# Cross-attention and a feed-forward block: query rows on other partitions, whole key tables from TensorE, the second mask half copied on the chip, one product per turn of maxima, and a new order

## The reference, cut to what matters

```python
x = x + xattn(layernorm(x), ctx, mask)     # x: (2, 1024, 256), ctx: (2, 77, 256), 16 heads of 16
x = x + ffn(layernorm(x))

def xattn(x, y, mask):
    q, k, v = x @ Wq + bq, y @ Wk + bk, y @ Wv + bv
    att = einsum('bthd,bThd->bhtT', q, k) / 4
    att = softmax(att * mask - 1e10 * (1 - mask))
    return einsum('bhtT,bThd->bthd', att, v) @ Wo + bo

def ffn(t):                                # only expert 0 has weight; F = 1024
    z = t + relu(t @ w1[0] + b1[0]) @ w2[0] + b2[0]
    return layernorm(z) * gamma + beta
```

## Time and profile before

| | |
|---|---|
| median of 3 runs | 226.63 us |
| the profiled execution | 226.6 us, of which span 224.8 us |
| PE busy | 198.1 us (88%), 1264 instructions |
| DVE, ACT, POOL busy | 148.7, 119.8, 80.8 us |
| DMA moved | 23.99 MB in 14267 packets |
| chain that ended last | PE 65%, DMA 18%, SyncE's queue 7% |

### The profile page before, as it was taken

The page is one execution under the profiler, slowest core; times in us unless marked ns, Lnnn a source line. Parts: engine busy times, 40 slices in busy tenths (PEclk is TensorE's granted clock), DMA queues, the critical chain, the costliest instruction groups (busy, mean ns, idle before and its releaser), DMA issues.

```text
span 224.8 us, 3534 instructions
## 1 busy us (share of the span) xinstructions
PE 198.1 (88%) x1264; PEld 153.4 (68%) x1264; DVE 148.7 (66%) x345; ACT 119.8 (53%) x216; POOL 80.8 (36%) x87
## 2 busy tenths in 40 slices
PE   0399979869968699798999999999999999999991
PEld 0376565437535557475879696667998899988990
DVE  0999999753936957454487219249664397895774
ACT  3298525826757085757725648986024960159200
POOL 4367952710000100598230104932245453371121
PEclk9999999967999999999999999999999999999999
DMA  6994498790999953995002230202000011010012
GB/s 216 382 358 141 152 242 187 140 260 0 208 211 230 211 130 73 156 175 110 5 1 74 71 70 4 73 0 96 0 0 3 0 48 47 3 47 0 3 70 70
DMA packets 14267, 23.99 MB, mean 107 GB/s; under 512 B 1716, under 2 KB 5300, under 8 KB 14250
## 3 DMA queue, kind: packets, MB, share of 16 engines
q1 hardware_dynamic: 13274, 22.71, 40.6%
q10 hardware_dynamic: 976, 1.06, 1.6%
HBM read 16.56 MB, written 6.55 MB: 103 GB/s over the span
## 4 chain that ended last, share of the span: by engine, by line
PE 65%; DMA 18%; SPq 7%; ACT 3%; issue 3%; DVE 2%; ACTq 0%; POOLq 0%; POOL 0%
DMA Sq<-nmx 7%; PE W L765 7%; PE W L768 6%; PE W L766 6%; PE acc L701 5%; PE W L751 5%; PE W L752 5%; PE W L753 5%; PE T L689 5%; DMA wk<-in_L_xattn_Wk_dram 3%; DMA wo<-in_L_xattn_Wo_dram 3%; DMA Sq<-qD 3%; PE M L668 2%; PE W L710 2%; DMA Mq<-qD 2%
## 5 line engine op out<-in xcount | busy, mean ns | idle before, releaser
L865 ACT ACTIVATE PT<-T 77x512 f32<-77x512 f32 x64 | 36.0, 591 | 21.8 <-PE T L689 20.2
L1005 DVE TENSOR_REDUCE mx<-M 128x6 f32<-128x462 f32 (+1 forms) x48 | 26.7, 579 | 19.9 <-PE M L668 19.7
L765 PE MATMUL W<-w2h,hh 128*128 128x256 f32 x128 | 36.6, 286 | 0.4 <-DVE aTl L1023 0.4
L768 PE MATMUL W<-w2h,hl 128*128 128x256 f32 x128 | 36.1, 282 | 0.0
L766 PE MATMUL W<-w2l,hh 128*128 128x256 f32 x128 | 36.1, 282 | 0.0
L689 PE MATMUL T<-Sq,KS 128*77 128x512 f32 x64 | 25.6, 431 | 7.7 <-DMA Sq<-nmx 5.5
L1180 POOL TENSOR_TENSOR hl<-hr,hh 128x512 fp32r<-128x512 f32 x12 | 16.1, 1338 | 43.6 <-ACT hh L911 43.6
L907 ACT ACTIVATE hr<-W,cst 128x512 f32<-128x512 f32 x32 | 22.0, 687 | 16.6 <-PE W L753 15.5
L751 PE MATMUL W<-x2h,w1h 128*128 128x512 f32 x64 | 25.8, 403 | 0.0
L765 PEld LDWEIGHTS W<-w2h,hh 128*128 128x128 f32 x128 | 24.1, 189 | 1.7 <-issue 1.5
L752 PE MATMUL W<-x2l,w1h 128*128 128x512 f32 x64 | 25.2, 394 | 0.0
(11 more groups left out here) (122 smaller groups left out, 407.9 us busy)
## 6 DMA issues: line engine op xcount, KB each, us to landing
Sq<-qD SPq DMA_DIRECT2D x16, 256.0 KB
xin<-in_x_dram SPq DMA_DIRECT2D x4, 512.0 KB, 7.5
qD<-qh SPq DMA_DIRECT2D x8, 256.0 KB, 3.7
qD<-ql SPq DMA_DIRECT2D x8, 256.0 KB, 3.6
Sq<-qD SPq DMA_DIRECT2D x16, 128.0 KB
out_dram<-xn SPq DMA_DIRECT2D x6, 256.0 KB, 2.0
Mq<-qD SPq DMA_DIRECT2D x6, 192.0 KB, 4.8
w1raw<-in_L_ffn_w_dram SPq DMA_DIRECT2D x2, 512.0 KB, 11.3
```

The source lines that it names most:

```text
L765: e.matmul(y, hh[:, f, q:q + 128], w2h[:, f * E:(f + 1) * E], start=(f == 0), stop=False)
L768: i = e.matmul(y, hl[:, f, q:q + 128], w2h[:, f * E:(f + 1) * E], start=False, stop=(f == 7))
L865: e.activation(PT[:, m % 6, :], T[m % 2][0:TK, :], ACT.Exp).then_inc(exped, 1)
L1005: e.tensor_reduce(heads, M[(nth[step] - 1) % 2][:, 0:w * KP].rearrange("p (g h t) -> p g h t", g=1 if s < 2 else 2, t=KP)[:, :, :, 0:TK], ...
```

## The change

- The query rows move from partitions 64 to 111 to partitions 32 to 79 (`Q0`, `Q1`).
- `qD` holds three rows a query element: high, low, high. The high rows are written twice by one DMA (512 KB in place of 256), and each quad is loaded by one `Sq<-qD` DMA of 48 partitions in place of two.
- The key tables are made whole by TensorE: a bfloat16 unit product (12 new matmuls of 468 or 312 columns) starts each group, and the selection products, now 128 partitions wide, add the keys. The unit copies of ScalarE and GpSimd are gone; the copies out of PSUM cover 128 partitions. A small unit tile `eyer` is made by GpSimd.
- `mD` and its nine DMAs are gone; GpSimd copies the second mask half from `mT1` into the slots (six copies "maskm", eight "masks"). Three of the six "mslot" copies go from VectorE to GpSimd.
- "mxt" is one matmul with a negated unit matrix in place of four transposes. `nmx` then has 32 partitions of 128 and its DMA moves 16 pieces of 512 B in place of 4 of 2 KB.
- The first 512 KB of x come in two halves, one on SyncE's queue and one on ScalarE's ahead of `cst`; `wo` and `b2` are loaded early.
- `TIMES` is new for every engine.

The diff, cut to its core (of `TIMES` two lines):

```diff
-Q0 = 64
-Q1 = 112
+Q0 = 32
+Q1 = 80
...
-        "mslot": "15.0 15.5 16.0",
-        "maskm": "49.7 56.0",
+        "maskm": "43.3 45.2 48.4 49.1 50.2 51.0",
...
-        qD = [dram(f"qD{c}", (H, D, 2, 512)) for c in range(NC)]
+        qD = [dram(f"qD{c}", (H, D, 3, 512)) for c in range(NC)]
...
-            e.dma_start(xin[:, 0:4, :], x_v[:, row0(0)]).then_inc(ld_x[0], 16)
+            e.dma_start(xin[:, 0:2, :], x_v[:, row0(0), 0:2]).then_inc(ld_x0[0], 16)
...
-                    for p, q in ((0, Q0), (Q1, MR)):
-                        e.dma_start(Mqf[p:q, first:first + n, :], mD[p:q, :].unsqueeze(1).to_broadcast([q - p, n, 512])
-                                    ).then_inc(ms_new[i], 16)
...
-                    e.dma_start(qD[c][8 * g:8 * g + 8, :, 0, :].rearrange("h d n -> (h d) n"),
-                                qh[:, 2 * (c % 2) + g, :].bitcast(F32)).then_inc(qh_out[2 * (c % 2) + g], 16)
+                    e.dma_start(qD[c][8 * g:8 * g + 8, :, 0:3:2, :].rearrange("h d r n -> (h d) r n"),
+                                qh[:, 2 * (c % 2) + g, :].bitcast(F32).unsqueeze(1).to_broadcast([P, 2, 512])
+                                ).then_inc(qh_out[2 * (c % 2) + g], 16)
...
-                    e.dma_start(Sqf[Q0:Q0 + 32, s:s + 4, :], heads.rearrange("h d r n -> (d r) h n")).then_inc(sq_ld[u % 2], 16)
-                    e.dma_start(Sqf[Q0 + 32:Q1, s:s + 4, :],
-                                heads[:, :, 0, :].rearrange("h d n -> d h n")).then_inc(sq_ld[u % 2], 16)
+                    e.dma_start(Sqf[Q0:Q1, s:s + 4, :], heads.rearrange("h d r n -> (d r) h n")).then_inc(sq_ld[u % 2], 16)
...
-                    e.dma_start(Sqf[MR:MR + 1, s:s + 4, :], source.bitcast(F32)).then_inc(sq_ld[u % 2], 16)
+                    e.dma_start(Sqf[MR:MR + 1, s:s + 4, :].rearrange("p h (n t) -> p (h n) t", n=4),
+                                nmx[4 * s:4 * s + 16, k // 2, :].bitcast(F32)).then_inc(sq_ld[u % 2], 16)
...
+                    e.matmul(t[:, 0:2 * KP * len(heads)], identb[:, :], eyer[:, 0:2 * len(heads), :],
+                             start=True, stop=False)
...
+                            made = e.matmul(o, sel_m[:, h, :], high, start=False, stop=last)
...
-                    for n in range(4):
-                        i = e.transpose(t[0:r, n * 128:(n + 1) * 128], mx[:, c % 2, n, r * g:r * g + r], ident)
-                    i.then_inc(mx_turned, 1)
+                    e.matmul(t[0:32, 0:P], mx[:, c % 2, 8 * g:8 * g + 8, :].rearrange("p h n -> p (h n)"), identn[:, :],
+                             start=True, stop=True).then_inc(mx_turned, 1)
...
+            e.dma_start(xin[:, 2:4, :], x_v[:, row0(0), 2:4]).then_inc(ld_x0[1], 16)
             e.dma_start(cst[:, :], const).then_inc(ld_c, 16)
...
+                elif kind == "maskm":
+                    i, = a
+                    fresh.wait_ge(mT_made, 2)
+                    fresh.wait_ge(scored, nth["smax", 1, 3, (0, 2, 1)[i // 2]])
+                    e.tensor_copy(Mq[:, FREED[i], :], mT1[:, :].bitcast(F32)).then_inc(ms_new, 1)
+                elif kind == "masks":
+                    s, = a
+                    fresh.wait_ge(mT_made, 2)
+                    fresh.wait_ge(st_made, nth["st", 1, 8 + s])
+                    e.tensor_copy(Sq[:, s, :], mT1[:, :].bitcast(F32)).then_inc(sq_new, 1)
```

More of the change, by code:

```diff
@@ L139, in members @@
 def members(kind):
-    if kind in ("consts", "eyem", "sel", "flags", "crow", "bqr", "bk4", "mask", "splitwo", "statics"):
+    if kind in ("consts", "eyer", "sel", "flags", "crow", "bqr", "bk4", "mask", "splitwo"):
         return [[(kind,)]]
@@ L146, in members @@
         return [[(kind, to, g, j) for to in ("KM", "KS") for g in range(2) for j in range(3)]]
-    if kind in ("late", "ksid", "mslot", "sslot", "maskm", "masks"):
-        return [[(kind, i) for i in range({"late": 2, "ksid": 4, "mslot": 6, "sslot": 8, "maskm": 2, "masks": 2}[kind])]]
+    if kind in ("late", "mslot", "sslot", "maskm", "masks"):
+        return [[(kind, i) for i in range({"late": 4, "mslot": 6, "sslot": 8, "maskm": 6, "masks": 8}[kind])]]
     if kind == "split":
@@ L153, in members @@
     if kind == "mxt":
-        return [[(kind, c, g) for g in range(turns(c))] for c in range(NC)]
+        return [[(kind, c, g) for g in range(2)] for c in range(NC)]
     if kind in ("qproj", "qlow", "qload", "attn"):
@@ L168, in members @@
     return [[(kind, c)] for c in range(NC)]
-def turns(c):
-    return 2
-def turned_by(c, k):
-    return sum(turns(i) for i in range(c)) + (k // 2 + 1 if turns(c) == 2 else 1)
 def pool_takes(step):
@@ L206, in has_part @@
     if step[0] == "mslot":
-        return (step[1] < 3) == (engine == "DVE")
+        return (step[1] < MSLOT_POOL) == (engine == "POOL")
     if step[0] == "low":
@@ L212, in has_part @@
     return True
-KINDS = ("consts", "eyem", "sel", "flags", "crow", "bqr", "bk4", "kproj", "mask", "mT", "values", "ksid", "mslot", "sslot",
-         "keys", "split", "splitwo", "statics", "late", "maskm", "masks", "norm", "scale", "turn", "xbias", "qproj", "qlow",
+KINDS = ("consts", "eyer", "sel", "flags", "crow", "bqr", "bk4", "kproj", "mask", "mT", "values", "mslot", "sslot",
+         "keys", "split", "splitwo", "late", "maskm", "masks", "norm", "scale", "turn", "xbias", "qproj", "qlow",
          "qload", "smax", "mxt", "quadq", "quadm", "st", "pv", "weigh", "attn", "proj", "scale2", "turn2", "bias2", "ffn1",
@@ L290, in build @@
         ql = sb("ql", [P, 2, 512], F32R)
-        mx = sb("mx", [P, 2, 4, H])
-        nmx = sb("nmx", [H, 2, 512], F32R)
-        PT = sb("PT", [TK, 6, 512])
+        mx = sb("mx", [P, 2, H, 4], F32R)
+        identn = sb("identn", [P, P], F32R)
+        mT1 = sb("mT1", [P, 512], F32R)
+        with ExitStack() as over:
+            sel_m, sel_h, sel_l = (over.enter_context(nc.sbuf_tensor(name, [P, 8, P], F32R))
+                                   for name in ("sel_m", "sel_h", "sel_l"))
+        PT = sb("PT", [P, 6, 512])
+        nmx = PT[96:P, 0, 0:256].bitcast(F32R).rearrange("p (g t) -> p g t", g=2)
         pvq = sb("pvq", [P, 2, 512])
@@ L346, in build @@
         K3 = [T[0], T[1], acc]
-        ld_x = [sem(f"ld_x{c}") for c in range(NC)]
+        mT = [mT0, mT1]
+        ld_x0, ld_x = [sem("ld_x0a"), sem("ld_x0b")], [None] + [sem(f"ld_x{c}") for c in range(1, NC)]
         ld_c, ld_ctx, ld_wk, ld_m = sem("ld_c"), sem("ld_ctx"), sem("ld_wk"), sem("ld_m")
@@ L563, in sync_program @@
                     u, s = quad(c, k), 4 * (k % 2)
-                    fresh.wait_ge(nmx_made, turned_by(c, k))
+                    fresh.wait_ge(nmx_made, nth["mxt", c, k // 2])
                     if u < 2:
@@ L607, in tensor_program @@
                     fresh.wait_ge(mT_made, half(c) + 1)
-                    e.matmul(t[:, :], bqr[:, g, :], mT[:, 512 * half(c):512 * half(c) + 512],
-                             start=False, stop=True).then_inc(q_made, 1)
+                    e.matmul(t[:, :], bqr[:, g, :], mT[half(c)][:, :], start=False, stop=True).then_inc(q_made, 1)
                 elif kind == "kproj":
@@ L781, in scalar_program @@
                 kind, a = step[0], step[1:]
-                if kind == "eyem":
-                    fresh.wait_ge(ld_c, 16)
-                    for k in range(2):
-                        i = e.copy(KM[:, 8 * k:8 * k + 8, :, :].rearrange("p h b t -> p (h b) t"),
-                                   eye.unsqueeze(1).to_broadcast([P, H, KP]))
-                    i.then_inc(km_ident, 1)
-                elif kind == "sel":
+                if kind == "sel":
                     fresh.wait_ge(ld_c, 16)
```

168 lines of the change are left out of this document (76 added, 92 removed), and 176 rows, old and new, of the table TIMES.

## The result

The changed kernel takes 211.51 us (median; 210.56 to 213.06), the kernel before, run beside it, 226.22 us (225.75 to 226.74). The ratio is 0.9356, with a 95% interval from 0.9294 to 0.9418. The forecast was 216.5 us with a range from 212.0 to 222.8: the direction was right, the size was not, and the time lies half a microsecond under the range. The profiled execution of the changed kernel took 211.6 us, 209.8 of it span, against 226.6 and 224.8 before.

What follows compares the result with a forecast made beforehand. TensorE bound the kernel, with a DMA-bound middle before a solid tail from 110 us. 226.6 + 1.2 (work) - 8.3 (DMA waits) - 3.0 (clock) + 0 (start) = 216.5 us, range 212.0 to 222.8.

Steps and rivals of the forecast that it cites:

- The DMA waits: TensorE's waits for loads into `Sq` and `Mq`: of 10.6 us, 2.3 stay, so -8.3 us (-10.6 to -4).
- Start: Wait for `wk` grows by 0.5 us behind x; the mask's turn pays it back: net 0 (-1 to +2).
- TensorE's work, +1.2: Unit products +2.2 us, wider selection products +1.2, "mxt" -2.2: sum +1.2 us (0.5 to 2.0).
- The half that the forecast drew: Quad loads on partitions 32 to 79: by the skill's port counts, half the time and the sum 1 us lower.
- Clock, -3.0: Idle gap of 2.53 us for `Mq<-qD` goes, and with it the clock's fall: -3.0 us (0 to -3.4).
- VectorE, nothing: VectorE loses three copies, but TensorE's wait was not for these; counted as nothing.
- GpSimd's copies, nothing: Fourteen mask copies, 9.6 us, hide where GpSimd is busy 1.02 of 22 us; counted as nothing.
- 1.72 us alone: VectorE's four scalings: said to take 1.72 us alone and 3.69 us with GpSimd at work.
- the lock: Rival: GpSimd's copies hold VectorE through the shared ports, its maxima come late for TensorE; 226.1 us, chance 0.04.
- everything lands in time: Rival: all DMA loads and small fills land in time, early VectorE waits go too; 212.3 us, chance 0.08.
- The early gap stays: Rival: chunk 1's `Mq<-qD` stays late, clock falls again, only stretches from 58 us gain; 222.3 us, chance 0.18.
- The signposts: Signs named: no gap over 1 us, clock at 9, DMA share well under 1.0 from 58 to 102 us.

Runs made afterwards that it cites:

- run 4: Kernel before with only the mask's second half moved from DMAs to fourteen GpSimd copies; 217.25 us, ratio 0.9667.
- run 15: Changed kernel's code walked in the kernel before's order, only the new steps put in; 217.49 us, ratio 0.9677.
- run 1: Changed kernel with only the query rows put back on partitions 64 to 111; 216.84 us, ratio 0.9677.
- run 7: Changed kernel with each of the 12 unit products made twice; 213.97 us, ratio 0.9496.
- run 2: Changed kernel with the mask's second half written to DRAM and loaded by eight DMAs again; 226.83 us, ratio 1.018.
- run 3: Kernel before with chunk 1's second pair of `Mq<-qD` issued ahead of the third quad's load; 225.43 us, ratio 0.9987.
- run 8: Changed kernel with the third quad's load put back ahead of the second pair of `Mq<-qD`; 215.17 us, ratio 0.9517.
- run 12: Kernel before with the mask by GpSimd and the second pair of `Mq<-qD` ahead of the third quad's load; 219.66 us, ratio 0.9845.
- run 6: Changed kernel with three mslot copies on VectorE again in place of GpSimd; 211.83 us, ratio 0.9416.

## Why the forecast was right in kind and wrong in size

Where the gain comes from, by medians:

| kernel | us | DMA waits | clock falls behind a gap |
|---|---|---|---|
| before | 226.2 | 10.6 | 3.4 of loss |
| before, mask by GpSimd (4) | 217.3 | 2.8 | 1.7 of loss |
| changed code, old order (15) | 217.5 | 2.9 | none |
| changed, rows on 64 to 111 (1) | 216.8 | 4.9 | none in the middle |
| changed | 211.5 | 1.2 | none |

The mask off the queue brings 7.5 us by the ratio of run 4 and 9.0 by these medians. The new rows, the whole tables, the single product and the split load of x bring nothing more in sum while the order is the old one; the single product was not tried by itself. The new order brings the last 5 to 6 us, and it does so with the new rows: with them back on 64 to 111, 5.3 us are lost.

**The step that failed** is in "The DMA waits" and "Start": the forecast priced the order as the move of one pair of loads, whose gap and clock fall it let go, and nothing else. It let 2.3 us of DMA waits stay, took the start for 0, and counted nothing for VectorE. Together that is the kernel of run 15, not the changed one: forecast 216.5 us, run 15 profiled 216.9 (median 217.5). What the runs showed in its place: the same code takes 217.5 us in the old order and 211.5 in the new. The gap and the clock's fall, which the forecast laid to the order, did not need it once the rest was changed: in run 15, with the loads in their old places, the gap before those maxima is 1.1 us, not 2.53, and the clock does not fall. So the forecast spent the order on a loss that the emptier queue took away too, and put the rest of the order's worth at nothing. A searched order moves every wait on TensorE's path before 100 us, and the forecast read the order only at one place. Term by term:

- *TensorE's work, +1.2.* The mechanism was right, its parts were mis-sized. The selection products take 0.04 us more each (0.11 against 0.07) where 0.02 to 0.03 was taken, 1.9 us in place of 1.2; the unit products 2.1 at full rate in place of 2.2 (run 7); the turned maxima save 8 x 0.30 = 2.4 in place of 2.2. By these spacings that is +1.6. In place, by the times from start to start with the start's half rate taken off (an estimate), the key products grew by 3.0 us and the turned maxima shrank by 2.5: +0.5.
- *DMA waits, -8.3.* Measured -9.4, 1.1 more. Of this -7.8 is the mask alone (run 4: 10.6 to 2.8). A quad's load saves 30% by its slots (1.3 us against 1.85, run 1), near the third that was taken, but against the kernel before's 1.55 us it saves 0.25, not 0.5. The Trainium skill, "SBUF — State Buffer", section "Door 1: The DMA port swizzle", has DMA bandwidth go by the number of ports reached, twelve against eight; that would be two thirds of the time (an estimate from that page), and the trace agrees. The half that the forecast drew from it needs the time to go by the four ports that are loaded twice, which no run here shows.
- *Clock, -3.0.* Measured -3.4 between the two profiles. Right, and the reason fits: no gap over 1 us after the start, no fall. Runs 2, 3, 4, 8 and 12 each show a gap and a fall with it. But a gap does not settle it (below), and the fall is not in every run of the kernel before: the mean granted clock of its 63 single runs lies between 0.963 and 0.998, and the four at 0.994 or more took 220.7 to 223.3 us. That one fall was priced and one was found is in part luck.
- *Start, 0.* With the order old, the weights' product waits 1.1 us longer with x rows ahead of `wk` (10.1 against 9.0), at the middle of the 0 to 2 that was named. The mask's turn, moved to before the weights, took this idle time back and 0.6 more. The forecast did not see that the earlier start puts more work into the half rate, about 1.2 us.
- *VectorE, nothing.* Measured -1.3. In the old order 1.1 us of it stayed; it is the order, not the three copies that moved to GpSimd (run 6).
- *GpSimd's copies, nothing.* Right: in run 4 the waits for VectorE stayed at 1.5 us with all fourteen copies in, and a maximum took 0.579 us before and 0.582 after. The row behind the forecast's "1.72 us alone" was misread: GpSimd was busy for 0.60 of these 1.72 us, and for all of the 3.69. By the lock that the Trainium skill states for the shared pair of ports ("SBUF — State Buffer", section "SBUF: two separate sides") the worst case was 9.6 us; the section binds it to VectorE operations in a two-port mode or with two inputs in SBUF, which leaves out the maxima, whose one input is in PSUM. No run here shows any of it on TensorE's path.

Between the forecast of 216.5 us and the profiled 211.6 lie 4.9: 1.1 of DMA waits, 1.3 of VectorE, 0.6 of idle time at the start, 0.6 of small waits, 0.4 of the clock, and 0.9 of busy time. Without the clock's fall the busy time rose by 0.3 us (-3.1 + 3.4), not by 1.2: +0.5 for keys and maxima, +1.2 for the start's half rate, and -1.4 in small pieces of the other products, which were not taken apart.

Of the rivals, "everything lands in time" (212.3) came nearest. Its condition was nearly met (1.2 us of DMA waits and 0.2 for VectorE stayed), and its chance of 0.08 was too low: a search of the order works on all of these waits at once. That its number is off by 0.8 us only is in part luck, since its +1.2 of work and its start of 0 were off too. "The early gap stays" is a real mechanism, one displaced DMA away (run 8), but at 215.2 us and not at 222.3.

The signposts held: the key weights' first product was at 9.39 us ("near 9.4"), no gap over 1 us, the clock at 9, the DMA share at 0.53 and 0.20 in the two stretches. The key products grew by 3.0 us where 3.4 was named.

## What to carry to other kernels

When a change takes load off a full queue and comes with an order found anew, price the parts in the old order first, and then give the order a term of its own, with all remaining waits of the bounding engine before its solid tail as the upper bound: here 14 us of waits in the old order (run 15), of which the search took 4.3 and 1.0 in smaller pieces. A single swap of two transfers tells little about it, since in a full queue the lateness passes to the next in line, and a transfer put behind a waiting one leaves the queue idle first. Where rows move to other partitions, look at how many pieces the copies that fill the tables fall into: a copy cut in pieces costs the full time of each piece.
